# A table's one-hots made by two VectorE instructions of half the chunks instead of one

## The reference: what is computed

```
e = jnp.stack([tbl_0[ids[:, 0]], ..., tbl_31[ids[:, 31]]], axis=1)
gram = jnp.einsum('bnd,bmd->bnm', e, e)      # upper triangle -> 496 values
h = jnp.concatenate([z, dense_ctx], axis=1)
h = jnp.maximum(h @ W_top1 + b_top1, 0.0)    # 512 -> 512
h = jnp.maximum(h @ W_top2 + b_top2, 0.0)    # 512 -> 256
y = h @ W_top3                               # 256 -> 1
```

## Time and profile before

| | |
|---|---|
| median of 3 runs | 494.22 us (491.78 to 495.32) |
| the profiled execution's own time | 495.87 us |
| its span, first to last instruction | 493.6 us |
| PE / DVE / ACT / POOL busy | 88% / 61% / 23% / 83% of the span |
| mean granted TensorE clock | 0.959 |

### The profile page before, as it was taken

How to read it: one execution, slowest core, us unless ns; L and a number is a source line. 1 busy time by engine, 2 the same in 40 slices (tenths; PEclk the granted TensorE clock), 3 DMA queues, 4 the chain that set the end, 5 groups by cost and what they waited for, 6 DMA issues and landing times.

```text
span 493.6 us, 10400 instructions
## 1 busy us (share of the span) xinstructions
PE 432.1 (88%) x4200; PEld 387.7 (79%) x4200; DVE 302.9 (61%) x369; ACT 114.2 (23%) x206; POOL 407.9 (83%) x522
## 2 busy tenths in 40 slices
PE   5298889989799989978999699988999679984987
PEld 5287789989598889877988599777988679874765
DVE  2499969968672698267925586366935847340400
ACT  2244313122012221231123110321113201230322
POOL 7999889999998899999988999889988999884110
PEclk9699999999999999999999899988999979995999
DMA  4534751012311222112311231122211231121010
GB/s 109 144 139 150 215 136 31 16 20 62 87 37 23 47 60 80 21 44 57 86 23 32 54 101 20 23 54 71 62 23 31 51 106 17 23 43 34 7 39 1
DMA packets 21814, 29.32 MB, mean 59 GB/s; under 512 B 9782, under 2 KB 14070, under 8 KB 20640
## 3 DMA queue, kind: packets, MB, share of 16 engines
q1 hardware_dynamic: 12980, 18.96, 11.3%
q0 software_dynamic: 8384, 8.60, 11.2%
q10 hardware_dynamic: 404, 1.09, 0.6%
HBM read 24.35 MB, written 0.07 MB: 49 GB/s over the span
## 4 chain that ended last, share of the span: by engine, by line
POOL 82%; issue 9%; PE 4%; DMA 2%; SPq 1%; DVE 1%; ACT 1%; DVEq 0%
POOL rows L253 59%; POOL pause L260 22%; PE mlp_ps L328 1%; PE gram_ps L316 1%; SPq L192 1%; PE mlp_ps L338 1%; DVE folded L530 1%; DMA rows<-tbl,index 0%; ACT folded L441 0%; PE gram_ps L352 0%; SPq L219 0%; DMA pairs<-dense 0%; DMA pairs<-folded 0%; DMA index<-ids 0%; PE turn_ps L289 0%
## 5 line engine op out<-in xcount | busy, mean ns | idle before, releaser
L253 POOL DMA_INDIRECT rows<-tbl,index x256 | 293.8, 1148 | 44.5 <-issue 42.1
L303 PE MATMUL turn_ps<-split_sb,onehot 125*128 125x192 bf16 x2272 | 213.5, 251 | 22.9 <-DVE split_sb L544 11.7
L303 PEld LDWEIGHTS turn_ps<-split_sb,onehot 125*128 125x128 bf16 x2272 | 193.7, 100 | 33.7 <-DVE split_sb L544 15.5
L495 DVE TENSOR_TENSOR onehot<-place,codes_wide 125x2048 bf16<-125x2048 f16 (+1 forms) x131 | 174.2, 1331 | 7.1 <-DMA place<-ids_scratch 7.1
L260 POOL MEMSET pause<- 128x384 f32 x256 | 111.5, 436 | 0.2
L503 DVE TENSOR_REDUCE rows<-turn_ps 128x128 f32<-128x384 f32 x128 | 71.1, 556 | 54.0 <-PE turn_ps L303 31.1
L530 DVE COPY_PREDICATED folded<-second_sb,gram_ps 128x512 f32<-128x512 int32 x64 | 46.7, 730 | 82.9 <-issue 47.7
L316 PE MATMUL gram_ps<-emb_t 64*128 64x128 f32 x1024 | 76.4, 288 | 3.7 <-DVE folded L530 2.2
L316 PEld LDWEIGHTS gram_ps<-emb_t 64*128 64x128 f32 x1024 | 63.8, 191 | 19.1 <-issue 14.8
L441 ACT COPY folded<-gram_ps 128x512 f32<-128x512 f32 x64 | 37.6, 587 | 150.4 <-PE gram_ps L316 132.3
L328 PE MATMUL mlp_ps<-pairs,w_sb 128*128 128x256 f32 x256 | 58.5, 383 | 1.2 <-DMA pairs<-dense 1.2
(11 more groups left out here) (28 smaller groups left out, 75.7 us busy)
## 6 DMA issues: line engine op xcount, KB each, us to landing
place<-ids_scratch SPq DMA_DIRECT2D x8, 1000.0 KB
rows<-tbl,index POOLq DMA_INDIRECT x256
pairs<-folded SPq DMA_DIRECT2D x122, 32.0 KB
emb_t<-tbl SPq DMA_DIRECT2D x8, 250.0 KB
folded<-tbl SPq DMA_DIRECT2D x5, 312.5 KB
w_sb<-w SPq DMA_DIRECT2D x1, 1024.0 KB
place<-ids_scratch ACTq DMA_DIRECT2D x1, 750.0 KB
rows<-tbl SPq DMA_DIRECT2D x2, 312.5 KB
```

Of the source, the lines that this page charges most:

```text
L253: nc.gpsimd.indirect_dma_start(rows[:, s % 2, slot, t, :], None, tables[f][:, :], bass.IndirectOffsetOnAxis(index[:, s, t, f:f + 1], 0),). ...
L303: last = nc.tensor.matmul(turn_ps[:, u % 2].rearrange("p k b -> p (k b)")[:, t * PARTS * DIM:(t + 1) * PARTS * DIM], onehot[:, u % RING, c ...
L495: nc.vector.tensor_tensor(onehot[:, u % RING, 0:SPAN[u], :], place[:, parity, u, :].unsqueeze(1).to_broadcast([TP, SPAN[u], SUPER]), codes ...
```

## The change

`make_onehot` issues two comparisons in the place of one, each over half the table's chunks (4 of 8, or 5 of 10): the first writes chunks 0 to half-1, the second the rest. Only the second counts `onehot_ready` up, so TensorE and SyncE wait for the same event as before. Nothing stands between the two. The elements compared, the buffers and every other instruction stay.

```
+assert all(span % 2 == 0 for span in SPANS)
...
-                nc.vector.tensor_tensor(onehot[:, u % RING, 0:SPAN[u], :],
-                                        place[:, parity, u, :].unsqueeze(1).to_broadcast([TP, SPAN[u], SUPER]),
-                                        codes_wide[:, CODE_AT[SPAN[u]]:CODE_AT[SPAN[u]] + SPAN[u], :],
-                                        ALU.is_equal).then_inc(onehot_ready, 1)
+                half = SPAN[u] // 2
+                for c in (0, half):
+                    code = CODE_AT[SPAN[u]] + c
+                    last = nc.vector.tensor_tensor(onehot[:, u % RING, c:c + half, :],
+                                                   place[:, parity, u, :].unsqueeze(1).to_broadcast([TP, half, SUPER]),
+                                                   codes_wide[:, code:code + half, :], ALU.is_equal)
+                last.then_inc(onehot_ready, 1)
```

## The result

The changed kernel takes 498.39 us (median of 4 runs, 497.88 to 500.03), the kernel before 493.0 us (490.95 to 495.32) on the same chip: ratio 1.0114, 95% interval 1.0057 to 1.0171. It is 1.1% slower, where 3.3% faster was forecast. The profiled execution took 498.84 us, its span is 497.1 us. Lines behind the diff have moved: gathers L254, pause L261, one-hot halves L499, sums L507, fold L534, `take_high` L543, `low` L548.

A forecast was written before the change was run, and what follows sets the result against it. POOL's unbroken stream of gathers and pauses was taken as the bound. Terms -14.8 - 2.4 + 2.5 - 1.4 = -16.1 took 495.87 to 479.8 us, 1.65 above the median: 478.1 us, 3.3% faster, range 472 to 490.

The forecast's parts named there:

- POOL's stream bounds the kernel: Whole kernel: POOL's gathers (59%) and the pauses behind them (22%) make 81% of the chain that ended last.
- The cost of a split on DVE: Each one-hot split costs DVE 0.05 us, 7 to 9 us over 131 one-hots, hidden, so zero on the path.
- Sixteen of sixteen: Prologue seams of one-hot and L539: all sixteen waiting gathers get in, so gathers should get in between two halves too.
- The walk for the prologue: Prologue, 6.8 us of gather waits: some gathers let in sooner, six tables lose 0.05 to 0.07 each, together -2.4 us.
- Gram stretches: Seven stretches, one in each step 0 to 6, 50 gathers with 26.5 us of waits: 56% goes, -14.8 us.
- the rest: Transposes and late gram batches, 16.5 us of waits: 0.07 us charged for each of some 36 short waits, +2.5 us.
- The walked stretch: One gram stretch followed gather by gather with halves: its seventh gather ends 2.27 us sooner, of 4.07 us of waits.
- The last wait: TensorE's wait for the last rows, 7.86 us before, shrinks to about 3 us.
- the clock: TensorE's half clock after the last wait: full clock would save some 2.8 us; between 0 and -2.8, -1.4 was taken.
- A: Rival, chance 0.14: the second half keeps gathers out, some 98 waits get 0.05 to 0.07 longer, +5.9, 500.1 us.
- B: Rival, chance 0.13: TensorE becomes the bound if a split costs DVE 0.15 us; gain about -8, 486 us.
- C: Rival, chance 0.11: gathers let in early meet the next one-hot, only single early entries count: -5, 489 us.

The follow-up runs named there:

- e8: The changed kernel with whole one-hots in the prologue and the pause cut from 384 to 192 elements in all steps: 577.69 us, ratio 1.1702.
- e1: The changed kernel with whole one-hots in the prologue, halves in all later steps: 484.7 us, ratio 0.9834 to the kernel before.
- e2: The changed kernel with halves in the prologue alone, whole one-hots in all later steps: 507.82 us, ratio 1.0325 to the kernel before.
- e9: The changed kernel with a one-element-a-partition DVE memset in the prologue, between the second half and the next table's `take_high`: 483.72 us, ratio 0.9814.
- e10: The changed kernel with a one-element-a-partition DVE memset in the prologue, behind `low` and ahead of the sum: 483.67 us, ratio 0.9797.
- e7: The changed kernel with whole one-hots in the prologue and step 0's pause cut to 192 elements: median 484.62 us, too spread for a ratio.

## Why the prediction was wrong

- **POOL's stream bounds the kernel, and a gather gets in 0.83 after the end of the DVE instruction that it meets**: right for both kernels (81% of the chain are the two lines of POOL, before and after); in e8 POOL is not the bound any more.
- **The cost of a split on DVE, 0.05 us**: 0.07. The prologue's period went from 3.34 to 3.41 us a table, and DVE's busy time grew by 8.6 us. It lies on no path but that of the prologue, where 0.07 x 16 is 1.1 us at most. By the Trainium skill ("VectorE: DVE Perf Modes", section on the TRN2 errata) it would be an estimated 0.157 us; the rows have less than half of that, and they decide.
- **"Sixteen of sixteen meet such a pair, and all get in. I take it that they get in"**: this step failed, and it alone turned the sign. The sixteen were all of two kinds, ten behind a gather without a wait and six behind one let in at a seam. The kind that the halves bring about, behind a gather let in at a sum, had no case in the trace of before; it is passed over in all of its 11 cases of the prologue after. (Five of nine behind a fold are passed over too, in the later steps.) The walk for the prologue was right for 8 us (gathers of 1.21 and 1.07, 1.81 apart, until the first sums), then eleven gathers in a row took 2.07 to 2.81 each: +13.1 in place of -2.4, an error of 15.5 us. e1 and e2 show the place, e9 and e10 that the loss goes when the chain has another instruction in it, although DVE then does more; the full condition is not known (e7).
- **Gram stretches and the rest, -14.8 + 2.5**: measured -10.6 in the changed kernel, -11.0 in e1. The walked stretch gave -2.06 for -2.27. The term was mis-sized by 1.7 us. The mechanism was right for the most part; the five gathers that were passed over between halves, some 0.74 us each, are the failed step again, and how much of the gap they make was not taken apart.
- **The last wait shrinks to about 3 us, the clock gives 1.4**: neither, and the 1.4 was a choice between 0 and 2.8 that no row decided. With the last gather 10.4 us earlier in e1, TensorE starts on the last rows 10.5 earlier (440.41 for 450.89), and still after 6.28 us of waiting (7.86 before), at the lower of its two levels again (0.50, 1.2 GHz):

```profile
439.50:442.50 3.00, 2.09 (x10) 2.09 (x11) 0.69 (x1) 0.00 (x0) 0.00 (x0) 0.50 0.14 33
```

  The waits are no reserve that the gain is taken from: rows that come sooner in one step let TensorE begin the next sooner.
- **The sum without the failed step**: e1 is nearly the forecast without its prologue term, -14.8 + 2.5 - 1.4 = -13.7; of the 3.1 us between that and the -10.6 of the profiled executions the later steps' gathers make 1.3 (-11.0 in e1) and the clock 1.4, and most of the rest lies outside the span. The forecast's mean of 1085 ns for a gather is a slip beside this: its own gather terms (-14.7) make 1091. One profiled execution against the other has 485.26 - 495.87 = -10.6 us; the medians have -7.4, since the profiled execution of before lay 3.8 us above the median beside e1.
- **Rivals**: A had the right sign and a wrong mechanism: the second half does not bar gathers as such (in the gram stretches most get in behind the first half or the second), and what is lost is not 0.06 us for each of 98 waits but 1.1 to 1.9 us for each of eleven in a row (2.07 to 2.81 for 0.95). B did not come: DVE's sums wait for TensorE for 51.6 us in all, TensorE for the sums for 0.9 us. C may be seen in part, in the gap between the forecast for the later steps and what they gave; no run isolates it.

The Trainium skill ("SBUF — State Buffer", section on SBUF's two separate sides) has a lock held for one instruction, and the traces agree. It also gives the ports to whichever operation starts first. There the trace of the changed kernel differs: the gather of 50.97 asks at 51.10, while L543 starts at 51.40 and has them first. What orders the two no run here says.

## What to carry to other kernels

Cutting a long instruction to let another engine in pays where the pieces stand between instructions that do not hold the shared resource, and can cost where they lengthen an unbroken chain of holders: look at what follows the chain, and at whether the waiter's own period brings it back to the same place each time. A count such as "sixteen of sixteen" is worth as much as the kinds of cases in it: sort them by what came before, and ask whether the change makes a kind that is not among them. Here the split should be used outside the prologue alone, or with a tiny memset in the chain: 484.7, 483.72 and 483.67 us, 1.7 to 2.0% below the kernel before; between these three the intervals tell nothing apart.

## What was unexpected of the hardware

- A waiting gather of POOL is passed over at seams between two-input DVE instructions in 101 of 147 cases when its predecessor was let in as a PSUM-reading instruction followed (six of the 46 others are sorted there only by the recorded order), and in 1 of 519 otherwise. Being passed over costs up to 1.86 us a gather (2.81 for 0.95), and with a constant pause repeats itself at every table. Eight gathers of e7 and e8 that the rule would have passed over were let in, so its full condition is open.
- A DVE memset of one element a partition, recorded with 0.06 us and beside its neighbour, broke that cycle in either of two places and gave 14.7 us (483.7 for 498.4).
- A shorter pause behind each gather did not shorten the cycle (2.97 + 0.27 in place of 2.81 + 0.44), and in all steps it made the kernel 17% slower, with 30.8 us in which TensorE's look-ups waited for nothing that the trace shows.
